# Two attention layers and a dense mixture of experts: ScalarE's exponentials one place earlier, VectorE's normalised shares one collection earlier

## The reference

```python
edge_index = jnp.stack([src, dst])
x = x + _L0_gnn_ref(_layernorm(x), edge_index, W, att_src, att_dst, bias)
x = x + _L0_ffn_ref(_layernorm(x)[None], ...)[0]
x = x + _L1_gnn_ref(_layernorm(x), edge_attr_64, W1, W2, att_l, att_r, bias, src, dst)
x = x + _L1_ffn_ref(_layernorm(x)[None], ...)[0]

# graph attention, layer 0 (4 heads; layer 1 is alike with 1 head and edge features in the score)
e = jax.nn.leaky_relu(a_src[src] + a_dst[dst], NEG_SLOPE)
m = jax.ops.segment_max(e, dst, num_segments=N)
e = jnp.exp(e - m[dst])
alpha = e / jax.ops.segment_sum(e, dst, num_segments=N)[dst]
out = jax.ops.segment_sum(alpha[:, :, None] * h[src], dst, num_segments=N)

# dense experts, layer 1 (8 experts, all of them for every row)
w = jax.nn.softmax(feat @ Wr + br, axis=-1)
h = jax.nn.relu(_bn(jnp.einsum('bfd,edh->bfeh', x, W1) + b1, g1, be1, m1, v1))
h = jax.nn.relu(_bn(jnp.einsum('bfeh,ehk->bfek', h, W2) + b2, g2, be2, m2, v2))
y = jnp.einsum('bfeh,ehd->bfed', h, Wo) + bo
return jnp.einsum('bfed,fe->bfd', y, w)
```

## Time and profile before

| | us |
|---|---|
| median of 3 runs | 4750.13 |
| lowest and highest | 4743.02, 4752.10 |
| profiled execution | 4749.81 |
| its span, first to last instruction | 4748.1 |
| TensorE busy | 3401.8 (72%) |
| VectorE busy | 2688.4 (57%) |
| GpSimd busy | 2214.1 (47%) |
| ScalarE busy | 1539.8 (32%) |
| mean granted TensorE clock | 0.812 |

### The profile page before, as it was taken

One profiled execution on the slowest core, in us unless ns is written; L12 is line 12 of the kernel. 1 busy time (PEld: TensorE's weight loads), 2 busy tenths in 40 slices (PEclk: granted clock), 3 DMA queues, 4 the chain that ended last, 5 costly groups with the idle time before them and its releaser, 6 DMA issues. The chain is left out here.

```text
span 4748.1 us, 73243 instructions
## 1 busy us (share of the span) xinstructions
PE 3401.8 (72%) x16240; PEld 2620.6 (55%) x16241; DVE 2688.4 (57%) x8451; ACT 1539.8 (32%) x4325; POOL 2214.1 (47%) x2095
## 2 busy tenths in 40 slices
PE   5267667665776768884467766666558999999999
PEld 3144444444444557773245444444436888888887
DVE  7478888788887775555455556655555412222121
ACT  2233333333332203331133333333333333333333
POOL 0377777777776013227577777777750000000000
PEclk9676776777667559996667788888878999999999
DMA  3333333333336214443344444444461000000000
GB/s 100 80 95 93 94 94 95 95 94 94 93 94 78 90 34 158 157 132 102 95 105 106 106 105 105 106 106 105 106 84 57 7 5 6 4 6 6 4 7 7
DMA packets 382578, 369.58 MB, mean 78 GB/s; under 512 B 249324, under 2 KB 309388, under 8 KB 382242
## 3 DMA queue, kind: packets, MB, share of 16 engines
q0 software_dynamic: 107072, 272.84, 23.1%
q1 hardware_dynamic: 272774, 92.39, 8.1%
q10 hardware_dynamic: 2396, 0.84, 0.1%
HBM read 324.13 MB, written 41.59 MB: 77 GB/s over the span
## 5 line engine op out<-in xcount | busy, mean ns | idle before, releaser
L682 POOL DMA_INDIRECT g_G<-rows,g_pack x1856 | 1959.6, 1056 | 782.1 <-issue 496.4
L715 PE MATMUL bank<-g_G,g_MB 128*125 128x260 f32 x1856 | 718.4, 551 | 145.4 <-DVE acc L920 143.2
L786 ACT ACTIVATE g_mt_d<-bank,unode 125x256 bf16<-125x256 f32 x928 | 384.9, 465 | 898.5 <-PE bank L700 898.4
L715 PE MATMUL bank<-g_G,g_M 128*125 128x257 f32 x1856 | 612.8, 489 | 84.9 <-DVE acc L920 84.1
L715 PEld LDWEIGHTS bank<-g_G,g_MB 128*125 128x125 f32 x1856 | 486.4, 277 | 337.3 <-DVE g_G L935 152.0
L920 DVE SCALAR_TENSOR_TENSOR acc<-acc,g_c,bank 125x65 f32 (+1 forms) x2320 | 619.0, 316 | 88.9 <-DVE acc L920 83.3
L1360 DVE SCALAR_TENSOR_TENSOR X<-bank,e_cw,X 125x256 f32 (+1 forms) x400 | 175.2, 479 | 842.9 <-PE bank L1186 842.9
L1256 ACT ACTIVATE e_h<-bank,e_bi_c,e_sc_c 128x250 f32<-128x250 f32 x800 | 404.2, 556 | 556.8 <-PE bank L1177 419.7
L715 PEld LDWEIGHTS bank<-g_G,g_M 128*125 128x125 f32 x1856 | 441.4, 249 | 223.8 <-DVE g_M L938 89.6
L935 DVE TENSOR_TENSOR g_G<-g_G 128x1024 f32<-128x1024 f32 x232 | 283.1, 1221 | 191.4 <-ACT g_G L828 191.4
L1186 PE MATMUL bank<-e_w,e_h 128*125 128x256 f32 x1600 | 377.9, 379 | 3.1 <-ACT e_h L1256 3.1
(11 more groups left out here) (302 smaller groups left out, 4194.6 us busy)
## 6 DMA issues: line engine op xcount, KB each, us to landing
g_G<-rows,g_pack POOLq DMA_INDIRECT x1856
acc<-in_edge_attr SPq DMA_DIRECT2D x50, 531.2 KB
g_pack<-edge_pack SPq DMA_DIRECT2D x928, 2.0 KB
g_drow<-edge_dst SPq DMA_DIRECT2D x928, 1.0 KB
expert_out<-x_y SPq DMA_DIRECT2D x54, 256.0 KB
g_qe<-edge_q SPq DMA_DIRECT2D x464, 1.0 KB
rows<-acc SPq DMA_DIRECT2D x25, 253.9 KB
rows<-n_T SPq DMA_DIRECT2D x25, 251.0 KB
```

The lines of the kernel that those rows point to most:

```text
L682: nc.gpsimd.indirect_dma_start(G[:, r, q, :], None, rows_d[l], bass.IndirectOffsetOnAxis(ap=pack[:, r, q, 0:1], axis=0)).then_inc(S(p + f" ...
L715: mm_ = nc.tensor.matmul(sum_bank(u)[0:TN, 0:HW], left, G[:, rk, q, :], start=(c == 0), stop=(c == C - 1))
L786: ins = nc.scalar.activation(mt_d[:, v_ % 2, k * C:(k + 1) * C, :], bank[2 + v_ % 2][0:TN, k * UE:(k + 1) * UE].rearrange("p (e c) -> p c ...
```

## The change

In the attention's ScalarE stream the three lines of the exponentials (wait for te, activation Exp, signal `w`) move from behind the first `place` and `hit` to in front of them. In the dense experts' VectorE stream `normal_shares` of the next group moves from behind the collection at e = 5 (that is the collection of expert 4, the fifth) to in front of it. No instruction is added or removed, and TensorE's, GpSimd's and SyncE's streams are as before.

```diff
@@ attention, ScalarE's slot
+                        if two:
+
+                            act.wait_ge(S(p + "te"), i - 1)
+                            to = wt[:, r2, :, :] if l == 1 else G[:, r2, :, :].rearrange("p q (h w) -> p q h w", h=H)[:, :, :, DH]
+                            nc.scalar.activation(to, te[:, :, :], ACT.Exp).then_inc(S(p + "w"), 1)
                         place(0)
                         lower(3, U - 2)
                         hit(0)
-                        if two:
-
-                            act.wait_ge(S(p + "te"), i - 1)
-                            to = wt[:, r2, :, :] if l == 1 else G[:, r2, :, :].rearrange("p q (h w) -> p q h w", h=H)[:, :, :, DH]
-                            nc.scalar.activation(to, te[:, :, :], ACT.Exp).then_inc(S(p + "w"), 1)
                         lower(3, U - 1)
                         place(1)
@@ dense_experts, VectorE's slot
                         for e in range(NX):
+                            if follows(i) and e == 5:
+                                normal_shares(i + 1, 1 - r)
                             if e or late(i, 1):
                                 collect(i if e else i - 1, r if e else 1 - r, i * NX + e - 1, (e - 1) % NX)
@@
                                 if e == 4:
                                     shares(i + 1, 1 - r)
-                                if e == 5:
-                                    normal_shares(i + 1, 1 - r)
                                 if e == 7:
```

More of the change, by code:

```diff
@@ L820, in slot @@
                             nc.scalar.copy(LT[:, :], rowT_ps[:, P:2 * P]).then_inc(S(p + "LT"), 1)
-                        place(0)
-                        lower(3, U - 2)
-                        hit(0)
                         if two:
@@ L828, in slot @@
                             nc.scalar.activation(to, te[:, :, :], ACT.Exp).then_inc(S(p + "w"), 1)
+                        place(0)
+                        lower(3, U - 2)
+                        hit(0)
                         lower(3, U - 1)
```

## The result

The changed kernel takes 4697.33 us (median of 4 runs, 4685.91 to 4698.14), against 4747.86 for the kernel before (4 runs): ratio 0.9888, 95% interval 0.987 to 0.9907, so it is 1.1% faster. The forecast was 4705, its range 4668 to 4740. Executions come in a faster and a slower state, and the ratios here compare the faster ones alone, so a ratio is not always the quotient of the two medians beside it. The profiled execution took 4696.63 us, its span is 4694.9, which is 53.2 less than before.

A forecast was written before the change was run, and what follows sets the result against it. The prediction took a full gather queue to bound the attention and TensorE the dense stage. From 4750 us it subtracted 41 (dense experts), 3 (attention's ends) and 0 (gather holds), 4706, given as 4705, range 4668 to 4740.

The forecast's parts named there:

- The bound: Attention: GpSimd's gather queue is full end to end, gaps 0.305 us; VectorE's waits stand beside it, its wide instructions lengthen gathers.
- Dense experts, 24 x 1.7 = 41 us: Dense stage: moving the shares ahead removes TensorE's wait before L1152 in 24 groups, 1.7 us each, 38 to 42 in all.
- the upper value: Dense stage: each group gains 1.75 us with the 0.16 us overlap, 1.59 without; 1.7 was taken.
- The first groups, thought a risk: Dense stage: in the first three groups a VectorE finish between the shares' halves could lose the gain, 5 us at worst.
- Rival (d): Dense stage: the bubble at L1152 returns at another TensorE wait, so no change, 4747 us; chance 0.07.
- Attention, 3.3 us behind the last gathers: Attention: earlier steps count only once per layer, after the last gather, 2.3 us in layer 0 plus 1.0 in layer 1.
- Where the wide instructions fall, 0: Attention: shifted scalings meet gather starts as often as before, so no change, within 0.5 us a layer 0 slot.
- the 30 us that the range held for this: Layer 0: allowance either way for gather holds by shifted scalings, 0.5 us a slot over 58 slots.
- (a): Layer 0: first and second scalings catch a gather in nearly every slot, +70 us, 4776 us, slower; chance 0.04.
- (b): Layer 0: neither of the first two scalings catches a gather, -58 us, 4648 us; chance 0.05.
- the 12 us given: Layer 1: its holds of 0.5 us a slot move by 0.2 at most, 12 us either way.
- The rival (c): Attention: the gather queue is not the bound and moved steps pay in full, 191 us, 4515 us; chance 0.02.

The follow-up runs named there:

- exp_late: Changed kernel with the attention's exponentials moved behind the second hit, later than in the kernel before: 4727.67 us, ratio 0.9951 to the kernel before.
- quarter_scale_b: Changed kernel with each layer 0 scaling treating only 16 of a head's 64 columns, so work is left out: 4567.64 us, ratio 0.9608 to the kernel before.
- dense_only: Kernel before with only the dense experts' part of the change, the shares ahead of the fifth collection: 4709.46 us, ratio 0.9918.
- attn_only: Kernel before with only the attention's part of the change, the exponentials ahead of the first placing: 4735.18 us, ratio 0.9964.
- copy_last: Changed kernel with `gone` before layer 0's third scaling and, in both layers, the carried copy before the fourth: 4678.17 us; on the slower chip 5167.18.

## Why the prediction was right, point by point

**The bound.** Right. The queue with its gaps of 0.30 us sets the attention's time, before and after, and VectorE's waits are beside it: exp_late brought the waits back, 200 us of them, and cost 30 us, most of it holds; quarter_scale_b removed holds and gained them in full.

**Dense experts, 24 x 1.7 = 41 us.** Right: 41.2. It is made of 1.8 a group (45.45 to 43.63) and of one distance that gained nothing, because the clock rose later at the stage's start. The 1.8 is the gap of 1.59 and the overlap of 0.16 that stood in the text as the upper value; 0.07 more was not followed up. That cancelling is chance: in dense_only the first distance gained 1.5 (34.7 us against 36.2) and the fourth nothing (47.59 against 47.65), as the granted clock was 0.75 and 0.91 in two stretches of 5 us there, and the sum is again 41.2; in exp_late the first took 36.8 and the fourth 47.59, and the stage is 2 us longer. The first groups, thought a risk, gained nearly as much as the others (45.35 to 43.64 us). Rival (d), the bubble coming back at another wait of TensorE, did not happen.

**Attention, 3.3 us behind the last gathers.** The steps are right: the second scaling comes 3.11 us after the spread (3.1 predicted), TensorE's wait for the rows grew by 2.5 us a slot (about 2 predicted), and RS is the late one on VectorE, as the text had it. The sums end sooner behind the last gather by 3.8 us in layer 0 (predicted 2.3) and by 2.2 in layer 1 (1.0 predicted; 41.4 to 39.3). That these microseconds reach the time is not shown, for either layer: in dense_only, with the attention of before, the sums of the two layers end 48.9 and 40.5 us behind the last gather, so part of the difference is chance, and what follows varies by more (the table of the stretches).

**Where the wide instructions fall, 0.** The average came out right and was then rounded away. The text worked out that the first two scalings pay 1.0 us a slot before and 0.9 after. Before, they paid (25.8 + 33.6) / 58 = 1.02; now it is (30.7 + 21.6) / 58 = 0.90. The split behind the average was wrong, though: the first scaling was to pay 0.8 to 1.0 in some slots and up to 0.1 in the others, and it holds 56 gathers in 58 slots, 30 of them for 0.26 to 0.45 us, 19 for 0.66 and 7 for longer. That this averages to the predicted 0.5 is luck. The text then called 0.9 against 1.0 no change, which drops 0.1 x 58 = 6 us. Another 2.2 us came off the third, where the distances were taken as fixed. With 10 instead of 0 the forecast would have been 4696. The measured 10 lies within the 30 us that the range held for this, and attn_only, with the same attention code and 171.6 us of holds, shows that some 6 us of it can be chance. Neither (a), always caught, nor (b), never caught, happened: the second scaling holds 32 gathers now and 55 before, since it meets a gather's start in one kind of slot and misses it in the other.

In layer 1 the sum is the same by luck rather than by reason: the second scaling's holds went from 10.6 to 21.3 us, the first's from 4.3 to 0, and those of the incidences from 9.5 to 4.9. Its change stayed within the 12 us given.

**The rival (c), that the moved steps pay in full (4515 us)** falls with attn_only and exp_late.

The Trainium skill (SBUF — State Buffer, section "Who interferes with whom") infers that a tensor_tensor with both inputs in SBUF leaves descriptor generation alone. quarter_scale_b disagrees by 125 us of gather time: an indirect gather is held by just such an instruction, in float32 and, at the incidences, in bfloat16. The same section of the Trainium skill says that such an instruction contends with a GpSimd instruction that reads SBUF. These gathers read their row numbers (`g_pack`, a tile in SBUF), so the hold may be that rule at work, and the prediction was too quick to take exactly zero from the page. No run here separates reading the row numbers from making the descriptors.

## What to carry to other kernels

A long wait on an engine says nothing until one has looked at the stage's full queue: here removing 191 us of it gave 15 us with all else, and bringing 200 back cost 30. The gain was in the wait of the engine that had no other idle time, and there the gap's length, its count and the small overlap behind it give the sum within 1 us. Where an engine next to the bound slows it by overlap, shortening the overlapping instruction pays, and shifting it pays only as long as the next one does not land on a gather's start in its place, so follow every wide instruction of the string before placing one.

## What the hardware showed that was not expected

- A gather is held by whether it starts under the wide instruction, not by how much of it lies beside. Over layer 0 of the eight profiles with whole scalings on the faster chips, gathers that start up to 0.04 us after a scaling can be free (66 of them, 0.95 us), and those that start 0.025 us after it or later can be held; from 0.05 us on every one is, to 0.81 us or more behind the scaling's end, and one at 0.09 us takes 1.94. A few that start just before the first scaling take 2.1 us: they start under SEL (L996), which is followed by the scaling without a pause, and end 0.82 us after the scaling. One that starts 0.85 us after it (1022.36 behind 1021.51) still waits, to 0.82 after the scaling's end. A scaling that starts together with a gather takes up to 1.30 us instead of 1.22, so it hardly pays itself.
- The same kernel took 4750 us on one chip and 5207 on another; where one kernel was profiled on both (copy_last), all of the difference lies where gathers run. A gain from shorter gathers depends on that, the gain in TensorE's stage does not.
- TensorE's sums got shorter, though nothing in them was changed: mean 461 ns (574.0 us over 1856) with the exponentials early, 549 in dense_only, whose attention is that of before. The weight loads no longer wait for the scaling (`<-DVE g_G L935` 149.5 us there, 9.9 now), which is the likely reason; no run tests it by itself. It gave no time, since TensorE then waits for the rows. The groups of layer 0, the changed kernel's and then dense_only's:

```profile
L715 PE MATMUL bank<-g_G,g_MB 128*125 128x260 f32 x1856 | 574.0, 461 | 27.8 <-DVE acc L920 27.0 <-DVE g_G L935 0.6
L715 PEld LDWEIGHTS bank<-g_G,g_MB 128*125 128x125 f32 x1856 | 401.0, 229 | 171.9 <-issue 51.6 <-DVE acc L920 32.4 <-DVE g_G L935 9.9
```

```profile
L715 PE MATMUL bank<-g_G,g_MB 128*125 128x260 f32 x1831 | 704.6, 549 | 143.7 <-DVE acc L920 141.5 <-DVE g_G L935 1.5
L715 PEld LDWEIGHTS bank<-g_G,g_MB 128*125 128x125 f32 x1832 | 476.4, 275 | 331.4 <-DVE g_G L935 149.5 <-issue 59.5 <-DVE acc L920 16.7
```
